# GNN block on one Trainium2 core: where the inverse root between two attention layers is made, and the order of ScalarE, TensorE and GpSimd around it

## What is computed

```python
def _gat_layer(x, src, dst, W, b, a, g, beta, N, concat):
    h = x @ W.T + b
    score = s_src[src] + s_dst[dst]                 # h @ a[:d], h @ a[d:]
    e = jnp.exp(-jax.nn.leaky_relu(score, ALPHA))
    h_prime = jax.ops.segment_sum(e[:, None] * h[dst], src, num_segments=N)
    mu = jnp.mean(h_prime, axis=-1, keepdims=True)
    var = jnp.var(h_prime, axis=-1, keepdims=True)
    h_prime = (h_prime - mu) * jax.lax.rsqrt(var + LN_EPS) * g + beta
    return jax.nn.elu(h_prime) if concat else h_prime

heads = [_gat_layer(...) for i in range(8)]         # 64 features each
x = jnp.concatenate(heads, axis=1)                  # 512 features
out = _gat_layer(x, ..., W_out, ...)                # 256 features
```

## Time and profile before

| | us |
|---|---|
| median of 3 runs | 3296.31 (3293.35 to 3298.26) |
| the profiled execution's own time | 3294.2 |
| its span | 3292.4 |
| busy TensorE, VectorE | 2243.2 (68%), 1917.8 (58%) |
| busy ScalarE, GpSimd | 1738.7 (53%), 1928.0 (59%) |
| mean granted TensorE clock | 0.825 |

### The profile page before, as it was taken

One profiled execution on the slowest core, in us unless ns is written; L12 is line 12 of the kernel. 1 busy time (PEld: TensorE's weight loads), 2 busy tenths in 40 slices (PEclk: granted clock), 3 DMA queues, 4 the chain that ended last, 5 costly groups with the idle time before them and its releaser, 6 DMA issues. The chain is left out here.

```text
span 3292.4 us, 46358 instructions
## 1 busy us (share of the span) xinstructions
PE 2243.2 (68%) x14916; PEld 1669.3 (51%) x14916; DVE 1917.8 (58%) x4213; ACT 1738.7 (53%) x5133; POOL 1928.0 (59%) x1999
## 2 busy tenths in 40 slices
PE   6887778677758877343577777777767566655653
PEld 4785667567747766233343333333335445444542
DVE  8985788577747776222446666666686233333336
ACT  3995677578747776222334444344438344444444
POOL 1006666666666666666635656665645566666664
PEclk8998999799878999555688888888888777777776
DMA  2011111111141112111545656665641333333335
GB/s 60 1 41 40 40 44 43 43 45 45 45 47 44 45 44 53 47 46 47 58 140 160 169 164 173 169 170 157 168 104 33 87 92 89 91 89 90 90 90 77
DMA packets 114882, 270.48 MB, mean 82 GB/s; under 512 B 34543, under 2 KB 51670, under 8 KB 114646
## 3 DMA queue, kind: packets, MB, share of 16 engines
q0 software_dynamic: 89088, 245.53, 30.5%
q1 hardware_dynamic: 25558, 21.98, 2.1%
HBM read 250.96 MB, written 16.42 MB: 81 GB/s over the span
## 5 line engine op out<-in xcount | busy, mean ns | idle before, releaser
L435 POOL DMA_INDIRECT rows_near<-table_a,s_idx_S x464 | 474.1, 1022 | 286.0 <-issue 115.4
L435 POOL DMA_INDIRECT given<-table,s_idx_S x464 | 449.2, 968 | 301.5 <-issue 126.8
L1166 DVE TENSOR_TENSOR work<-work,bank 128x129 f32 (+2 forms) x928 | 391.0, 421 | 362.4 <-remote 163.1
L435 POOL DMA_INDIRECT rows_near<-table,s_idx_S x464 | 446.8, 963 | 252.7 <-issue 127.8
L435 POOL DMA_INDIRECT rows_near<-table_b,s_idx_D x464 | 450.0, 970 | 230.9 <-issue 101.9
L950 PE MATMUL bank<-scratch,oh 128*128 128x512 f32 x928 | 488.1, 675 | 15.9 <-DVE scratch L1413 11.7
L818 PE MATMUL bank<-rows_near,oh 128*128 128x129 f32 x1856 | 331.0, 330 | 246.6 <-issue 179.5
L647 ACT ACTIVATE e_att<-lrelu 128x32 f32<-128x32 f32 (+1 forms) x232 | 49.9, 215 | 740.6 <-DVE lrelu L1402 490.0
L818 PEld LDWEIGHTS bank<-rows_near,oh 128*128 128x128 f32 x1856 | 289.0, 234 | 282.1 <-issue 232.8
L935 PE MATMUL bank<-sort_ring,scratch 128*128 x2784 | 154.0, 169 | 329.4 <-ACT scratch L643 285.2
L538 ACT ACTIVATE scratch<-scratch,given 128x128 f16<-128x128 bf16 x840 | 284.1, 388 | 170.8 <-DVE scratch L1130 146.7
(11 more groups left out here) (222 smaller groups left out, 4799.8 us busy)
## 6 DMA issues: line engine op xcount, KB each, us to landing
rows_near<-table_a,s_idx_S POOLq DMA_INDIRECT x464
rows_near<-table_b,s_idx_D POOLq DMA_INDIRECT x464
rows_near<-table,s_idx_S POOLq DMA_INDIRECT x464
given<-table,s_idx_S POOLq DMA_INDIRECT x464
table<-scratch SPq DMA_DIRECT2D x25, 260.0 KB
table<-scratch SPq DMA_DIRECT2D x25, 128.5 KB, 3.0
xs<-in_x SPq DMA_DIRECT2D x1, 3072.0 KB
out_x<-scratch SPq DMA_DIRECT2D x24, 128.0 KB, 1.7
```

What stands on the lines that cost most here:

```text
L435: nc.gpsimd.indirect_dma_start(out=to, out_offset=None, in_=table[:, :], in_offset=bass.IndirectOffsetOnAxis(ap=s_idx[order][:, c:c + 1], ...
L1166: v.tensor_add(a, a, psum).then_inc(sum_free[o], 1)
```

## The change

`head_deviations` on ScalarE is gone, and with it the two semaphores of the root. VectorE makes the inverse root itself, by a bit shift, a multiply-add on integers and three Newton steps, 13 small instructions for a block, of which all but one pair wait for the one in front. For the first two blocks it does so beside the last turns of layer 1 (step 6 of `beside_heads`), and GpSimd scales these blocks as soon as it is told. TensorE's dense(n-2) becomes dense(n-1). ScalarE makes features(n-2) ahead of squares(n), not behind. On VectorE ELU(n-3) becomes ELU(n-2) and evacuation(n-5) becomes evacuation(n-4), ELU first. GpSimd centres block n, then scales block n-1 (before: scales n-2, then centres n).

```diff
 # GpSimd
+            def head_scaled(n):
+                pool.wait_ge(head_scales, n + 1)
+                for t in HEAD_BLOCKS[n]:
+                    ... nc.gpsimd.tensor_tensor(y, y, head_var[:, t, :]..., ALU.mult).then_inc(head_normed, 1)
+            for n in range(HEAD_EARLY):
+                head_scaled(n)
             for n in range(HEAD_EARLY, len(HEAD_BLOCKS) + 3):
-                if 2 <= n < len(HEAD_BLOCKS) + 2:
-                    pool.wait_ge(head_scales, n - 1)
-                    ... multiply the tiles of HEAD_BLOCKS[n - 2]
                 if n < len(HEAD_BLOCKS):
                     ... centre the tiles of HEAD_BLOCKS[n]
+                if HEAD_EARLY < n <= len(HEAD_BLOCKS):
+                    head_scaled(n - 1)
 # ScalarE
-            for n in range(HEAD_EARLY):
-                head_deviations(n)
-            for n in range(HEAD_EARLY, len(HEAD_BLOCKS) + 2):
+            for n in range(HEAD_EARLY, len(HEAD_BLOCKS) + HEAD_EARLY):
+                head_features(n - HEAD_EARLY)
                 if n < len(HEAD_BLOCKS):
                     for t in HEAD_BLOCKS[n]:
                         head_square(t)
-                if HEAD_EARLY < n <= len(HEAD_BLOCKS):
-                    head_deviations(n - 1)
-                if n >= 2:
-                    head_features(n - 2)
 # TensorE
-                for n in range(len(HEAD_BLOCKS) + 2):
+                for n in range(len(HEAD_BLOCKS) + 1):
                     if n < len(HEAD_BLOCKS):
                         head_transposes(n)
-                    if n >= 2:
-                        head_dense(n - 2)
+                    if n >= 1:
+                        head_dense(n - 1)
 # VectorE
+            def head_scale(n):
+                a, b = HEAD_BLOCKS[n].start, HEAD_BLOCKS[n].stop
+                dve.wait_ge(square_used, b)
+                x = head_var[:, a:b, :]
+                minus_half_x, y, s = [root_part[:, i, 0:b - a, :] for i in range(3)]
+                link(v.tensor_scalar(x, x, 1.0 / D, EPS, ALU.mult, ALU.add))
+                v.tensor_scalar(minus_half_x, x, -0.5, None, ALU.mult)
+                link(v.tensor_scalar(y.bitcast(I32), x.bitcast(I32), 1, None, ALU.logical_shift_right))
+                link(v.tensor_scalar(y.bitcast(I32), y.bitcast(I32), -1.0, float(ROOT_START), ALU.mult, ALU.add))
+                for i in range(ROOT_STEPS):
+                    link(v.tensor_tensor(s, y, y, ALU.mult))
+                    link(v.tensor_tensor(s, s, minus_half_x, ALU.mult))
+                    last = v.scalar_tensor_tensor(out=y if i < ROOT_STEPS - 1 else x, in0=s, scalar=1.5, in1=y, op0=ALU.add, op1=ALU.mult)
+                    if i < ROOT_STEPS - 1:
+                        link(last)
+                last.then_inc(head_scales, 1)
 # beside_heads
                     if 4 <= step < 6:
                         head_squares(two_tiles(n, step - 4))
+                    if step == 6:
+                        head_scale(n)
 # VectorE, behind layer 1
-            for n in range(HEAD_EARLY, len(HEAD_BLOCKS) + 5):
-                if 2 <= n < len(HEAD_BLOCKS) + 2:
-                    head_scale(n - 2)
+            for n in range(HEAD_EARLY, len(HEAD_BLOCKS) + HEAD_EARLY + 2):
                 if n < len(HEAD_BLOCKS):
                     head_sums(HEAD_BLOCKS[n])
                     head_means(n)
                 if HEAD_EARLY < n <= len(HEAD_BLOCKS):
-                    head_variances(n - 1)
-                if 3 <= n < len(HEAD_BLOCKS) + 3:
-                    head_elu(n - 3)
-                if n >= 5:
-                    for t in HEAD_BLOCKS[n - 5]:
+                    head_squares(HEAD_BLOCKS[n - 1])
+                    head_scale(n - 1)
+                if n < len(HEAD_BLOCKS) + HEAD_EARLY:
+                    head_elu(n - HEAD_EARLY)
+                if n >= HEAD_EARLY + 2:
+                    for t in HEAD_BLOCKS[n - HEAD_EARLY - 2]:
                         dense("2", C, 1, s_src2, tab_2, t)
```

More of the change, by code:

```diff
@@ L50 @@
 EPS = 1e-5
+ROOT_START = 0x5F3759DF
+ROOT_STEPS = 3
 ALPHA = 0.2
@@ L143, in build @@
         head_var = scratch2[:, at + T * HEADS:at + 2 * T * HEADS].rearrange("p (t h) -> p t h", h=HEADS)
+        root_part = scratch2[:, at + 2 * T * HEADS + 2 * HD:at + 2 * T * HEADS + 2 * HD + 12 * HEADS].rearrange("p (i t h) -> p i t h", i=3, t=4)
         xs = sb("xs", [P, T, C])
@@ L333, in build @@
         head_sum = sem("head_sum")
-        head_vars = sem("head_vars")
-        head_std = sem("head_std")
         head_scales = sem("head_scales")
@@ L504, in _ @@
             gather_layer1("1", table_1, W1)
-            for n in range(HEAD_EARLY, len(HEAD_BLOCKS) + 3):
-                if 2 <= n < len(HEAD_BLOCKS) + 2:
-                    pool.wait_ge(head_scales, n - 1)
-                    for t in HEAD_BLOCKS[n - 2]:
-                        y = work[:, t, :].rearrange("p (h d) -> p h d", h=HEADS)
-                        nc.gpsimd.tensor_tensor(y, y, head_var[:, t, :].unsqueeze(2).to_broadcast([P, HEADS, D]), ALU.mult).then_inc(head_normed, 1)
+            def head_scaled(n):
+                pool.wait_ge(head_scales, n + 1)
+                for t in HEAD_BLOCKS[n]:
+                    y = work[:, t, :].rearrange("p (h d) -> p h d", h=HEADS)
+                    nc.gpsimd.tensor_tensor(y, y, head_var[:, t, :].unsqueeze(2).to_broadcast([P, HEADS, D]), ALU.mult).then_inc(head_normed, 1)
+            for n in range(HEAD_EARLY):
+                head_scaled(n)
+            for n in range(HEAD_EARLY, len(HEAD_BLOCKS) + 3):
                 if n < len(HEAD_BLOCKS):
@@ L1449, in _ @@
             dve.wait_ge(sum_free["1"], GROUPS + 4)
[L1452 to L1456, removed]
             def head_elu(n):
@@ L1464, in head_elu @@
                     v.scalar_tensor_tensor(out=z, in0=exp_block(n, k)[:, 0:w], scalar=-1.0, in1=z, op0=ALU.add, op1=ALU.max).then_inc(z_made, 1)
-            dve.wait_ge(square_used, HEAD_BLOCKS[HEAD_EARLY].start)
-            dve.sem_inc(head_vars, HEAD_EARLY)
-            for n in range(HEAD_EARLY, len(HEAD_BLOCKS) + 5):
-                if 2 <= n < len(HEAD_BLOCKS) + 2:
-                    head_scale(n - 2)
+            for n in range(HEAD_EARLY, len(HEAD_BLOCKS) + HEAD_EARLY + 2):
                 if n < len(HEAD_BLOCKS):
```

## The result

The changed kernel takes 3324.53 us (3320.69 to 3329.17, 4 runs) where the kernel before takes 3294.83 us on the same chip (4 runs; the three of the table above gave 3296.31): 29.7 us more by the medians, ratio 1.0098 with a 95% interval of 1.0085 to 1.0110, which is 28 to 36 us. Forecast were 3328 (3308 to 3340) and a chance of 0.93 for slower.

A forecast was written before the change was run, and what follows sets the result against it. No engine above 68%; the 96.8 us stage behind layer 1 was read as a chain. Layer 1's loss, the front's gain and three 18.6 us turns moved its end from 2558.6 to 2590.7: +32, median 3328 us (3308 to 3340).

The forecast's parts named there:

- The ring (d): Behind layer 1: features, ELU, evacuation, dense product, transposes follow one another without overlap; 16.3 us a turn at full clock, against 12.5.
- The clock (e): TensorE's dense products behind idleness start at half clock; 2.3 us more for each of five, making a turn 18.6 us.
- Layer 1 (b): End of layer 1: two roots on VectorE cost 6.0 us, messages disturbed by GpSimd's scaling 4.0; 10.0 us later.
- The lock: VectorE's messages beside GpSimd's scalings in layer 1: if strictly exclusive, 8.1 us lost in place of 4.0.
- The front (c): Start behind layer 1: first transposes no longer wait for a root there; F(2) starts 2.5 us earlier.
- The table loads (a): ScalarE loses 12 table loads and seven roots, some 17 us; counts only if ScalarE stays the pace-maker.
- The sum: Whole stage, layer 1's end to last evacuation: all terms chained, ending at 2590.7 against 2558.6, +32 us.
- Rival 1: Closed chain of engines, but clock stays up (+20.5 us, 3317) or engines hardly disturb each other (+23); chance 0.18.
- Rival 3: Not slower: evacuation is in time, ScalarE's 9.6 us set the pace; -1 us, 3295; chance 0.07.
- Rival 2: All five dense products at 1.2 GHz throughout, +7.2 us each; +57 us, 3353; chance 0.05.

The follow-up runs named there:

- e1: Changed kernel, but TensorE makes dense(n-2) behind transposes(n) again, not dense(n-1); ratio to the kernel before 1.0017.
- e2: Changed kernel, but VectorE evacuates block n-4 ahead of ELU(n-2), not behind it; ratio to the kernel before 0.9999.
- e3: Kernel before, but TensorE makes dense(n-1) behind transposes(n), not dense(n-2); roots stay on ScalarE; ratio to the kernel before 1.0111.
- e7: Kernel before, but VectorE makes the inverse root by 13 instructions where the reciprocal stood, orders unchanged; ratio to the kernel before 1.0005.
- e4: Changed kernel, but GpSimd scales the first two blocks only after TensorE's last sums of layer 1; ratio to the kernel before 1.0106.
- e6: Changed kernel with first scalings after layer 1, VectorE order root(n-2), squares(n-1), ELU(n-3), evacuation(n-4), two Newton steps; ratio to the kernel before 0.9972.
- e10: Changed kernel with VectorE order root(n-2), squares(n-1), ELU(n-3), evacuation(n-4), first scalings after layer 1, three Newton steps; ratio to the kernel before 0.9977.
- e5: The filler run: changed kernel, with useless identity transposes on TensorE while it waits for the dense products; ratio to the kernel before 1.0063.

## Why the prediction was right

Points counted from the fixed point ahead of turn 113.

- **The ring (d)**, with the clock's price in it, was the cause: opening it at either of two places gives back 27 or 33 us where 32 had been lost (e1, e2), closing it in the kernel before costs 38 (e3). Dense products 1 to 4 were forecast 18.6 us apart and came 19.4, 18.2 and 19.4 us apart. With TensorE kept busy the turns are 16.6 to 16.9, for the 16.3 of full clock. The new orders on ScalarE and GpSimd have no run of their own; with everything else of the change they are in e1, which is 5.5 us slower than the kernel before.
- **The clock (e)**: 2.3 us for each of five dense products; they took 10.06, 8.91, 10.01, 8.88 and 8.88 for 7.22, mean +2.13, and each began at 0.50. The filler run removes it and takes 10.3 us off the stage.
- **Layer 1 (b)**: forecast 10.0 us, measured 10.9 (26.5 - 15.6). Two roots took 2.63 us each for the 3.0. Two groups of messages took 5.03 each for the 4.50, so the price from the ELU's row was too low by 0.5 each time. The rest, 0.6, has no term in the sum: a small VectorE instruction behind the first group (L1412) took 0.81 us in place of 0.19, beside GpSimd's last scaling.
- **The lock**: beside each other, messages and scalings both start every 1.45 us, where alone they start every 0.60 and 1.00 us; 5.03 is 0.68 + 3 x 1.45. The two engines nearly take turns, and a message waits 0.85 us for a scaling. By that, the exclusive lock of the Trainium skill (SBUF — State Buffer, "Who interferes with whom") is how these rows behave, but for 0.15 us of each pair of 1.60. The 8.1 that I had made of it was too high: the first message goes ahead, so three wait and not four, and they wait 0.85 and not 1.0 (2 x 3 x 0.85 = 5.1).
- **The front (c)**: F(2) forecast at 49.1, measured 50.3 (51.6 before). The root beside GpSimd: forecast +1.5, measured +1.4 (its first two instructions take 0.76 and 0.97, the small ones elsewhere 0.17 to 0.19). So 1.3 us are won at the front, not 2.5: scaling(2) took 5.77 for the 4.9, and transposes(2) ran at 0.50.
- **The table loads (a)**: their removal, paid with Newton steps on VectorE, is worth nothing in the kernel before (e7). But (a) says that it counts only while ScalarE sets the pace, and that is too narrow: in the closed ring the features stand in each turn, and with their load in it the turns are 20.5 us (e3) and not 18.2 to 19.4. The sum was not hurt, because its 7.4 us of features are without the load.
- **The sum**: the stage was forecast 32 us longer and is 32.3 longer. The medians' difference is 29.7; 0.98% of 3294.83 is 32.3. That it comes this close is luck in part. Layer 1 ended 0.9 us late, but a root beside GpSimd took 4.0 us for the 4.5, and dense(1), to which VectorE's list leads and not F(2), started at 62.8 for 62.7; then three turns took 57.0 for 55.8, and the end behind them 24.9 for 26.0.
- **Rival 1** (ring without the clock's price, +20): its condition was made true by the filler run, which measures +22 in the stage. **Rival 3** (evacuation in time, -1): e2 makes its condition true and measures -0.9, but the number agrees by luck in part: F(2) to F(6) came 18.1, 14.2, 10.4 and 8.9 us apart, not all 9.6. **Rival 2** (all of dense at 1.2 GHz) didn't occur: the granted clock over each of the five was 0.71 to 0.81.

Where my expectations behind the prediction missed: later scaling (e4) was to give 3 to 5 us and gave none, since I had counted the end of layer 1 and not GpSimd's list behind it; the gains of e1, e2 and e6 were larger than expected; and e10 as told above.

## What to carry to other kernels

When engines work through lists in a fixed order, draw for each resource that is reused (a bank, a ring of buffers) who frees it and behind what that stands in the freeing engine's list; moving one step a block closer can turn two engines that overlap into two that alternate, and a turn is then the sum of their times (here 7.4 of features and 7.2 of dense product, and what lies between) where it was the longer list alone, however much busy time was saved elsewhere. Free buffers ahead of work that has to wait, not behind it. And look at who pays for work that is removed: here 17 us less on ScalarE against 21 us more on VectorE left the time as it was.

## What the runs showed of the hardware

- Useless matmuls in the gaps made the stage 10 us shorter: with them the granted clock was 1.00 in all five dense products, without them 0.71 to 0.81 behind 4.3 to 10.0 us of idleness. A wait of 1.46 us in front of a dense product (e2) left it at 7.22, one of 3.52 us cost 1.7. But the last wait alone doesn't decide: one of 2.13 us cost 1.7 as well in the kernel before, behind transposes that had waited too, and one of 3.17 us behind the useless work cost nothing (e5, dense(1), 7.21).
- The cost of such a product came in two sizes, 8.9 and 10.0 us for equal work behind equal waits of 7.59 us. In the longer ones the granted clock stayed at 0.50 for longer: it was still 0.50 from 2.2 to 5.2 us after the start of dense(3) (10.01 us), and 0.74 from 1.9 to 4.9 us after that of dense(4) (8.88 us).
- 13 small VectorE instructions on 128 x 32 elements take 2.63 us; those that wait for the one in front start 0.21 to 0.23 us after it.
- The kernel before took 3295 us in one group of runs and 3327 to 3331 in three others. Why is open.
